# Two attentions and two feed-forwards on 16 sequences: scores as fp32 products in row tiles of TensorE, operations 1024 wide, and a written-out order

## What is computed

```python
x = x + _L0_xattn_ref(_layernorm(x), ctx_2048, ctx_2048)   # 16 heads of 16, causal, softmax over 128 keys
x = x + _L0_ffn_ref(_layernorm(x), base_w, base_b, router_w, router_b, lora_A, lora_B)   # linear + top-2 of 8 LoRAs
x = x + _L1_xattn_ref(_layernorm(x), ctx_2048, ctx_2048, gamma)   # 8 heads over x transposed: 256 queries, 256 keys, width 16
x = x + _L1_ffn_ref(_layernorm(x), w1, w2, gamma)   # rms norm, 8-bit rounding, ternary w1, exact gelu, ternary w2
```

## Time and profile before

| | us |
|---|---|
| median of 3 runs | 398.62 |
| lowest, highest | 397.15, 402.47 |
| span of the profiled execution | 399.2 |

### The profile page before, as it was taken

How to read it: one execution, slowest core, us unless ns; L and a number is a source line. 1 busy time by engine, 2 the same in 40 slices (tenths; PEclk the granted TensorE clock), 3 DMA queues, 4 the chain that set the end, 5 groups by cost and what they waited for, 6 DMA issues and landing times.

```text
span 399.2 us, 9590 instructions
## 1 busy us (share of the span) xinstructions
PE 306.1 (77%) x2926; PEld 192.0 (48%) x2946; DVE 315.5 (79%) x841; ACT 262.4 (66%) x501; POOL 271.7 (68%) x508
## 2 busy tenths in 40 slices
PE   0355665867989999898898899998777866767884
PEld 0233543654655656556555465555344432444553
DVE  6543579589898889899895889987797657999993
ACT  2422434636766887869576786596457548997993
POOL 5763988988988898699996795654542133756555
PEclk9999589869899999999998999999898889698998
DMA  5777768875866569567775667523444000000112
GB/s 185 188 222 225 185 168 253 240 177 159 187 183 201 153 180 251 152 196 175 203 218 129 187 160 203 132 64 84 96 108 118 14 16 1 0 16 29 40 54 79
DMA packets 73138, 56.21 MB, mean 141 GB/s; under 512 B 5376, under 2 KB 62592, under 8 KB 73088
## 3 DMA queue, kind: packets, MB, share of 16 engines
q1 hardware_dynamic: 69888, 51.67, 48.4%
q10 hardware_dynamic: 3200, 3.93, 3.3%
HBM read 36.45 MB, written 18.87 MB: 139 GB/s over the span
## 4 chain that ended last, share of the span: by engine, by line
PE 28%; POOL 19%; DVE 15%; issue 14%; DMA 12%; SPq 6%; ACT 4%; POOLq 1%; ACTq 0%; DVEq 0%
PE ps_u L1244 6%; DMA q<-max_t 5%; DVE max L1851 5%; PE ps_st L1213 4%; DMA kv_in<-in_kv 3%; PE ps_s L1197 3%; PE ps_ff L1314 3%; SPq L628 2%; POOL p L920 2%; POOL xs L1116 2%; PE ps_st L1182 2%; DMA k_parts<-k_split 2%; POOL rstd L970 2%; DVE hq L2302 1%; POOL k_split L853 1%
## 5 line engine op out<-in xcount | busy, mean ns | idle before, releaser
L1851 DVE TENSOR_REDUCE max<-ps_s 128x2 f32<-128x512 f32 (+1 forms) x192 | 127.0, 682 | 33.6 <-PE ps_s L1166 17.0
L1565 ACT ACTIVATE p<-ps_st 128x512 f32<-128x512 f32 x128 | 71.7, 599 | 18.7 <-PE ps_st L1213 16.9
L1213 PE MATMUL ps_st<-q,k 98*128 98x256 bf16 x256 | 47.9, 284 | 9.4 <-DMA q<-max_t 4.7
L1197 PE MATMUL ps_s<-k,q 96*128 96x256 bf16 x256 | 50.2, 283 | 5.4 <-DVE max L1851 2.5
L920 POOL TENSOR_SCALAR_AFFINE_SELECT p<-p 128x512 f32<-128x512 f32 x64 | 39.7, 636 | 8.1 <-ACT p L1555 8.0
L1555 ACT ACTIVATE p<-ps_st 128x512 f32<-128x512 f32 x64 | 35.6, 601 | 13.1 <-PE ps_st L1182 12.3
L1244 PE MATMUL ps_u<-p,v 128*32 128x256 f32 x512 | 38.0, 419 | 5.7 <-POOL v L910 5.7
L1213 PEld LDWEIGHTS ps_st<-q,k 98*128 98x128 bf16 x256 | 20.1, 100 | 31.5 <-DMA q<-max_t 9.2
L1166 PE MATMUL ps_s<-k,q 96*128 96x128 bf16 x256 | 27.2, 232 | 7.2 <-POOL p L920 6.4
L1569 ACT ACTIVATE q_split<-xs,shift,rstd 128x256 bf16<-128x256 f32 (+1 forms) x32 | 22.7, 711 | 12.4 <-POOL shift L972 8.1
L1081 POOL TENSOR_SCALAR amax_c<-amax,rms 128x1 f32<-128x1 f32 x16 | 4.9, 305 | 37.4 <-DVE amax L2256 37.3
(11 more groups left out here) (144 smaller groups left out, 800.3 us busy)
## 6 DMA issues: line engine op xcount, KB each, us to landing
k_parts<-k_split SPq DMA_DIRECT2D x16, 512.0 KB, 4.8
k<-k_parts SPq DMA_DIRECT2D x32, 256.0 KB, 3.6
q<-q_parts SPq DMA_DIRECT2D x32, 256.0 KB, 4.0
kv_in<-in_kv SPq DMA_DIRECT2D x16, 256.0 KB, 3.9
q_parts<-q_t SPq DMA_DIRECT2D x16, 256.0 KB, 3.5
k<-k_parts SPq DMA_DIRECT2D x32, 128.0 KB, 3.6
q<-q_parts SPq DMA_DIRECT2D x32, 128.0 KB, 4.0
q_parts<-q_split SPq DMA_DIRECT2D x16, 256.0 KB, 3.1
```

What stands on the lines that cost most here:

```text
L1197: last = pe.matmul(out_[:, f * D:(f + 1) * D], q[0:STK, odd, h * D + f * P:h * D + (f + 1) * P], k[0:STK, odd, h * D:(h + 1) * D], start=( ...
L1213: last = pe.matmul(out_[:, f * D:(f + 1) * D], k[0:STM, odd, h * D + f * P:h * D + (f + 1) * P], q[0:STM, odd, h * D:(h + 1) * D], start=( ...
L1565: act.activation(p1[:, h, :], ps_st[bank_of(ST_BANKS, f"s1t{h}")][:, :], ACT.Exp, scale=SCALE).then_inc(exp1_done[h], 1)
L1851: dve.tensor_reduce(out_, src, AX.X, ALU.max, negate=True).then_inc(done, 1)
```

## The change

The program is written anew around the scores:

- q and k stay fp32. k comes straight from the input in DRAM into tiles of 32 partitions, each with two heads of 16 channels; where head e sits, the other head's rows are zero. A head pair is one matmul with 32 rows; there are four such row tiles (`I = 4`), and scores of half of them (`HALF = 2`) go to two banks at once. The stacks, the splits of q and k and `k_parts`, `q0_parts`, `q1_parts` are gone. SP issues 8 small loads for `k0` and 8 for `k1` per batch.
- The maxima are split on GpSimd, transposed in four bf16 transposes, and enter the transposed scores as a bf16 matmul with two rows of ones per row tile, instead of through a DMA into the stack.
- `ps_s` and `ps_st` are one pair of banks each, 1024 columns: reductions, Exps and masks are 1024 wide, six reductions and six Exps a batch instead of twelve each. A new round claims the pair as a whole.
- `together` lays the matmuls of up to two rounds (one of `s`, one of `st`) alternately, by columns.
- `x1_`, `index_f`, `pick2_` and the splits of maxima go from DVE to GpSimd.
- Weights, x and constants are all loaded by SP, w1 and w2 first; zeroing of k0, k1 and the splits is new on DVE.
- `up` writes `ps_ut` and `ps_u`, `turn_hid` writes `ps_ut`; seven buffers for hidden rows and transposed inputs. All Gelus stand after the last Exp.
- Orders of steps are lists of calls with batch numbers, without loops.

```diff
-PARTS = 3
-STK = 6 * DH
-STM = STK + 2
+R = 32
+I = P // R
+HALF = I // 2
+E = R // DH
+BANK = 512
...
-        ps_s = [bank(f"ps_s{i}", [P, G * P]) for i in range(2)]
-        ps_st = [bank(f"ps_st{i}", [P, G * P]) for i in range(2)]
+        ps_s = bank("ps_s", [P, HALF, BANK])
+        ps_st = bank("ps_st", [P, HALF, BANK])
...
+            def load_k0(b):
...
+                for i in range(I):
+                    for e in range(E):
+                        rows = slice(i * R + e * DH, i * R + (e + 1) * DH)
+                        sp.dma_start(k0[rows, n, :, e, :],
+                                     kv[b, rows, 0, :].rearrange("p (f l) -> p f l", f=FT)).then_inc(k0_landed[n], 16)
...
+            def together(*streams):
+
+                moved = {s: 0 for s in streams}
+                while moved:
+                    least = min(moved, key=moved.get)
+                    columns = next(least, None)
+                    if columns is None:
+                        del moved[least]
+                    else:
+                        moved[least] += columns
...
+            def scores0(b, h):
+                n = b % K0_BUFS
+                claim("s")
+                for m in range(HALF):
+                    pe.matmul(ps_s[:, m, :], ident_bf[:, :], mask_q[:, :, :].rearrange("p g k -> p (g k)"), start=True,
+                              stop=False, skip_group_check=True)
...
+                for f in range(FT):
+                    for m in range(HALF):
+                        i = h * HALF + m
+                        rows = slice(i * R, (i + 1) * R)
+                        last = pe.matmul(ps_s[:, m, f * D:(f + 1) * D], q0[rows, b % Q_BUFS, f, :],
+                                         k0[rows, n, f, :, :].rearrange("p e l -> p (e l)"), start=False, stop=True,
+                                         skip_group_check=True)
...
+                    yield D
...
+            def scores0_t(b, h):
...
+                for c in range(FT * E):
+                    f, e = c // E, c % E
+                    for m in range(HALF):
+                        i = h * HALF + m
+                        rows = slice(i * R, (i + 1) * R)
+                        pe.matmul(ps_st[:, m, c * P:(c + 1) * P], k0[rows, n, f, e, :], q0[rows, b % Q_BUFS, f, :],
+                                  start=(c == 0), stop=True, skip_group_check=True)
+                    yield P
+                for m in range(HALF):
+                    i = h * HALF + m
+                    pe.matmul(ps_st[:, m, :], ones_bf[i * R:i * R + 2, :],
+                              max0_t[i * R:i * R + 2, :, :].rearrange("p c q -> p (c q)"), start=False, stop=True,
+                              skip_group_check=True).then_inc(st0_ready[h], 1)
...
+            def scores1(b, f, h):
...
+                    pe.matmul(ps_s[:, m, :], q1[rows, b % Q_BUFS, f * P:(f + 1) * P],
+                              k1[rows, n, :, :].rearrange("p e l -> p (e l)"), start=True, stop=True,
+                              skip_group_check=True).then_inc(s1_ready[f][h], 1)
```

`scores1_t(b, k, h)` has two matmuls of 256 columns in each of its two row tiles and the same matmul of ones. One full period of the new order on PE (line by line, without the waits):

```diff
+            turn_max1(5)
+            pv1(4, 0)
+            together(scores1(6, 1, 1))
+            together(scores1_t(5, 0, 0))
+            pv1(4, 1)
+            turn_max0(9)
+            together(scores1_t(5, 0, 1), scores1(6, 1, 0))
+            turn_gated(7)
+            turn_u1(4)
+            together(scores0_t(9, 1), scores1(6, 0, 0))
+            turn_xh1(8)
+            lora(7)
+            together(scores0_t(9, 0), scores1(6, 0, 1))
+            turn_back(4)
+            ff(8)
+            together(scores1_t(5, 1, 1), scores0(10, 0))
+            pv0(9, 0)
+            pv0(9, 1)
+            turn_q0(11)
+            together(scores1_t(5, 1, 0), scores0(10, 1))
+            turn_u0(9)
```

Before the first such period the list has six batches of the first attention and two of the second, from the last on only the second attention's rounds; on SP it begins so:

```diff
+            load_weight(0)
+            load_x(0)
+            load_weight(1)
+            load_constants()
+            load_k1(0)
+            load_k1(1)
+            load_kv(0)
+            load_kv(1)
+            load_kv(2)
+            load_x(1)
...
+            load_x(5)
+            load_k0(0)
```

More of the change, by code:

```diff
@@ L256, in kind @@
[L256 to L265 removed]
+X_GROUPS = ((0, 1), (1, 2), (2, 4), (4, 6), (6, 10), (10, NB))
+KV_BUFS = 3
+K0_BUFS = 3
+K1_BUFS = 5
+V0_BUFS = 3
+V1_BUFS = 5
+Q_BUFS = 2
+XN_BUFS = 4
+XR_BUFS = 3
```

3849 lines of the change are left out of this document (2275 added, 1574 removed).

## The result

The changed kernel takes 430.46 us (median of 4 runs, 429.8 to 430.87) against 400.55 for the kernel before (4 runs, 397.15 to 403.21): 1.077 times as long, 95% interval 1.070 to 1.084. The forecast was 408, with 372 to 452 as its range. So the direction was right, but 9 us of loss were foretold and 30 came.

What follows compares the result with a forecast made beforehand. PE was taken as the bound, through mode changes and stalls, with DVE setting the fill. Start 25 + fill 80 + ten periods 190 + drain 49 + tail 64 = 408 us, range 372 to 452.

Steps and rivals of the forecast that it cites:

- The full period: Ten periods with both attentions' scores running: PE-bound, 19.0 us each (18.1 to 19.4), 190 in all.
- Stalls: Full period: after the third and fourth rounds too little PE work covers the 1.5 us reduction wait, 1.4 us of stall.
- The extra for matmuls of unlike length: Full period: in one in-order queue a second pass sits behind the longer matmul's first, up to 0.25 in each of five pairs.
- the forecast's sum of PE's work: Full period: scores and masks 8.1, the rest 6.3, 19 changes of tiling 2.3; 16.7 us a batch.
- 26 rounds with a reduction: Fill, first score to first full period: DVE's work of 66 us plus waits for PE, 80 (68 to 90).
- nine rounds wait for PE with nothing in between, 1.5 each: Fill: about nine rounds wait 1.5 us each, added to DVE's 66 us to give 80.
- PE waits for the maxima that went through GpSimd: Fill: DVE idle during this wait would be a sign of a fault there; no size given.
- 2.7 a round, 49: Drain, last period to last Exp: 18 rounds with little between, 1.2 and 1.5 each, 49 us (43 to 52).
- About 10.6: DVE's work per batch after the change, down from 13.83 us, so that DVE does not bind.
- D: Score matmuls: row tiles don't run together at all; period 32 us, total near 590; chance 0.04.
- B: Score rounds: row tiles' weight loads go one after another; 3.7 us a period more, 453 us; chance 0.20.
- C: Whole kernel faster: stalls filled, unlike matmuls undisturbed, tiling changes in waits; period 16.8, 363 us, halfway 385; chance 0.28.

Runs made afterwards that it cites:

- the two edits that add up to 17.78: Changed kernel with masks ahead of the pair (alone 424.6 us) and the wait for the copied maxima behind the score matmuls (alone 426.4 us).
- one pass: Changed kernel with score matmuls reading only the upper 16 bits of q and k, as bfloat16: 371.3 us in one run.
- the kernel of 409.2 us: Changed kernel plus masks ahead of the pair, late wait for the maxima, early first loads and PE kept busy in fill and drain: 409.2 us.
- that of 401.8: Kernel of the first step with k0(4), k0(5) loaded ahead of k1(2) to k1(4) and batch 1's maxima ahead of the first weight sum: 401.8 us.
- the first step: The kernel of 409.2 us with GpSimd's first rstd0 groups ahead of place_v0, x(1) ahead of k0(0), later statistics, fewer busy matmuls: 407.8 us.
- SP's order alone: Changed kernel with only SP's loads reordered, k0(4) and k0(5) ahead of k1(2) to k1(4): 434.1 us.
- the late wait alone: Changed kernel with PE's wait for the copied maxima moved behind the score matmuls, directly ahead of the matmuls with ones: 426.4 us.
- the best order: The order of the kernel of 409.2 us: masks ahead of the pair and late wait for the maxima, period 17.78 us.
- the kernel of 400.2 us: That of 401.8 with the MLP weights' sums, scales, roundings and clips moved out of the fill to later places: 400.2 us.

## Why the prediction was right in direction and wrong in size

**The full period: right in sum, not in parts.** 19.0 forecast, 18.99 measured. Stalls were put at 0.8 and 0.65, for a reduction, and are 0.51 and 0.41, for an Exp. The extra for matmuls of unlike length, 0.9 taken, does not exist: the long pairs are 1.29 and 1.31. In its place stand two costs that the forecast had not got: masks in the middle of a pair, which it counted as two changes of tiling (0.24), break the run of four tiles and cost 0.63 a pair, and a wait of 0.46 for the maxima, hidden behind a running neighbour. That errors of opposite sign met at 19.0 is luck. With both mended PE is busy for 16.70 us a period, and the forecast's sum of PE's work was 16.7. That PE's order of work sets the period is shown by the two edits that add up to 17.78.

**The fill: the step that failed.** "26 rounds with a reduction, DVE 66 us, nine rounds wait 1.5 each: 80". DVE's 66 was right (64.1). The step that failed is the term "nine rounds wait for PE with nothing in between, 1.5 each", 13.5 us: DVE idles 29.6 us there (93.64 - 64.09). The profile lists 21.9 of it as ten waits for the first attention's scores, the first begun before the fill. What DVE waits for is PE's score rounds. With one pass they are shorter, and the fill shrinks by 15.0 with DVE's work all but the same. The forecast took its list of rounds from DVE's side only and never summed PE's work there, 79.4 us. That sum alone would have given its 80 again. What neither sum holds is that the two engines wait for each other in turn: PE idles 14.3 us, 7.3 of them in four waits for the split maxima.

The forecast had named this last as the sign of a fault in the order ("PE waits for the maxima that went through GpSimd"). It is no such fault in the changed kernel: each of the four splits starts 0.14 or 0.15 us behind its reduction, so the wait is the length of the chain from reduction to transposes. Of waits for a load ahead of something urgent PE shows only the 1.06 us for k0(4) in this fill. The large ones, 10.7 us on GpSimd and 7.1 and 4.3 on PE, came up when the first loads were put in another order, and kept that from paying: the even periods begin at 116.2 in the kernel of 409.2 us and at 108.6 in that of 401.8, 7.6 us earlier, of which the first step brought 1.7; SP's order alone had brought none. The clock gave 1.8 there. The first load, moved, gave 3.7. How the 13.6 us of the miss divide among these was not shown.

**The start.** 25 forecast, 26.8 measured, and its price was not what was thought: making the first round 19 us earlier gained 3.7.

**The drain: mis-sized by the clock.** 2.7 a round, 49, was nearly right for PE at 2.4 GHz: 50.9 in the kernel that only keeps it busy, and 49.2 in that of 409.2 us, which has both edits of order too, each with a granted clock of 1.00 in the drain. With the clock at 0.89 and 0.81 it is 53.9 and 55.8. So about 3 of the 4.9 us are the clock's; the late wait alone took off 3.2 (50.7, at 0.92), and the parts don't simply add. The forecast used the rates of the full stretch throughout and never asked for the clock outside it.

**DVE.** "About 10.6" a batch is 13.89. `xn`, with the same shape, takes 1.00 us in the period where it took 0.57 in the first window of the earlier trace rows. The maximum over `xn`, its reciprocal and its scale, 0.79 together, are in the period but not in that window: in the kernel before they first run at 267.9. The forecast also subtracted durations of single operations from a union of overlapping records, which may take away too much; how much of the other 2.1 us that is I have not separated. It cost nothing here, because PE hid it.

**The rivals.** D is refuted by the pairs of 1.29 to 1.31. B asked for pairs of 2.1 where the loads of weights are most; 1.31 was measured. C asked for periods under 17.3; the best order reached 17.78, and a kernel level with before. What it lacks is the price of fp32 scores, 0.65 in such a pair, five pairs a period.

## What to carry to other kernels

Sum every stretch of a pipeline from the side of each engine, the fill and the drain too, and then follow one batch through it: where the engines work in turn, as here, the stretch (93.6 us) is longer than the largest sum (79.4), by the waits for each other. In hand-written orders look for instructions that wait for a DMA ahead of something urgent, on every in-order queue, and look again after each change of the order of loads: mended on one queue, the wait came up on the next. A wait put ahead of a group of matmuls although only the last of them needs it costs its full length, and no idle time shows it while a neighbour runs.

## What was not expected of the hardware

- Rounds in different row tiles overlap without being interleaved in the program, when nothing that takes the whole array lies between: 0.01 us between the starts of two rounds issued one behind the other. Interleaving brings most where the first round has many short matmuls (1.31 against 1.73; a round of longer ones first, 1.29 against 1.39).
- Two matmuls of the whole array in the middle of a four-tile pair cost 0.63 us beyond their own time, which they lose again when they stand ahead of it; two changes of tiling at the forecast's 0.12 would be 0.24.
- The granted clock of the page says 1.00 for 20 to 40 us in the changed kernel, but the records there are those of half the clock (2.08 for a round that takes 1.13 in the kernel that keeps PE busy). The length of the records is the surer sign here.
- The level differs between executions whose PE work is the same at that place. The drain of the kernels of 401.8 and 400.2 us has the same order, yet one profile has 1.00 and the other 0.72 and 0.77 between 300 and 320 us, and its drain is 2.9 us longer. In the kernel with the late wait the records are those of the lower level from 27 to 62 and from 69 to 76 us, in the changed kernel from 27 to 44 and from 54 to 61. Up to the first routing product its PE is busy for 41.9 us against 35.3, for the same matmuls, and idle for 9.3 against 10.1. So the moved wait added no idle time, and it is PE's longer records that make the 5.8 us; why the level fell stays open. By the Trainium skill, "TensorE: Matmul & The Clock Gate", Part 1, how much runs at the lower level after a start differs from run to run of one kernel. The executions here agree: nine of the kernel of 400.2 us took from 398.8 us at a mean granted clock of 0.994 to 403.3 at 0.979.
